# Interaction tower on one core: unrolled, row copies on VectorE, dots spread over the pairs, MLP feature by feature

## The reference

```python
e = stack([tbl_f[ids[:, f]] for f in range(32)], axis=1)   # [512, 32, 256], float32
z = einsum('bnd,bmd->bnm', e, e)[:, iu, ju]                # i < j: 496 dots per sample
h = concatenate([z, dense_ctx], axis=1)                    # 16 dense columns
h = maximum(h @ W_top1 + b_top1, 0)                        # 512
h = maximum(h @ W_top2 + b_top2, 0)                        # 256
y = h @ W_top3                                             # [512, 1]
```

## Time and profile before

| | us |
|---|---|
| median of 3 runs | 179.75 |
| lowest and highest | 179.70, 179.94 |
| profiled execution | 179.57 |
| its span | 177.8 |
| TensorE busy | 142.3 (80%) |
| GpSimd busy | 119.3 (67%) |
| VectorE, ScalarE busy | 61.5, 59.0 |

### The profile page before, as it was taken

How to read it: one execution, slowest core, us unless ns; L and a number is a source line. 1 busy time by engine, 2 the same in 40 slices (tenths; PEclk the granted TensorE clock), 3 DMA queues, 4 the chain that set the end, 5 groups by cost and what they waited for, 6 DMA issues and landing times.

```text
span 177.8 us, 3958 instructions
## 1 busy us (share of the span) xinstructions
PE 142.3 (80%) x1122; PEld 128.3 (72%) x1122; DVE 61.5 (35%) x185; ACT 59.0 (33%) x185; POOL 119.3 (67%) x131
## 2 busy tenths in 40 slices
PE   0387665797689999767689999767679999789995
PEld 0175554786569999646579999646579999678993
DVE  2101615045150255634140255534140255576202
ACT  2011415124150261533151162533151162565210
POOL 4777777777777777777777777777777777760000
PEclk9999999699999999999999999999999999999999
DMA  0356876533343333333333333333343333331000
GB/s 17 90 165 233 285 228 188 169 101 118 96 123 101 115 110 105 110 104 119 92 121 97 116 104 107 111 102 118 95 121 96 116 103 110 109 102 33 0 0 0
DMA packets 8801, 19.69 MB, mean 111 GB/s; under 512 B 2706, under 2 KB 3730, under 8 KB 8788
## 3 DMA queue, kind: packets, MB, share of 16 engines
q0 software_dynamic: 6000, 16.39, 31.0%
q10 hardware_dynamic: 1874, 2.69, 4.8%
q1 hardware_dynamic: 914, 0.46, 0.9%
HBM read 19.54 MB, written 0.00 MB: 110 GB/s over the span
## 4 chain that ended last, share of the span: by engine, by line
PE 51%; POOL 21%; DMA 14%; issue 9%; ACT 2%; DVE 1%; DVEq 0%; ACTq 0%
POOL rows L169 21%; PE gram_ps L191 18%; PE act_ps L239 12%; DMA rows<-tables,idx 10%; PE xt_ps L184 10%; PE dve_ps L239 4%; DMA w_sb<-w 3%; PE act_ps L250 2%; PE dve_ps L250 2%; PE act_ps L258 1%; PE xt_ps L234 1%; DMA ids_sb<-ids 1%; ACT xt L379 1%; DVE z L123 1%; ACT z L123 1%
## 5 line engine op out<-in xcount | busy, mean ns | idle before, releaser
L169 POOL DMA_INDIRECT rows<-tables,idx x125 | 118.6, 948 | 39.5 <-issue 29.6
L191 PE MATMUL gram_ps<-xt 128*128 128x128 f32 x512 | 71.4, 285 | 3.1 <-ACT xt L379 3.1
L184 PE MATMUL xt_ps<-ident,rows 128*128 128x128 f32 x250 | 47.5, 295 | 30.0 <-DMA rows<-tables,idx 26.5
L191 PEld LDWEIGHTS gram_ps<-xt 128*128 128x128 f32 x512 | 64.8, 199 | 4.8 <-ACT xt L379 4.0
L184 PEld LDWEIGHTS xt_ps<-ident,rows 128*128 128x128 f32 x250 | 29.0, 146 | 40.6 <-DMA rows<-tables,idx 29.2
L313 DVE COPY xt<-xt_ps 128x512 f32<-128x512 f32 x32 | 22.1, 692 | 83.8 <-PE xt_ps L184 83.5
L123 ACT COPY z<-gram_ps 32x64 f32 (+5 forms) x136 | 34.6, 254 | 36.1 <-PE gram_ps L191 34.7
L123 DVE COPY z<-gram_ps 32x64 f32 (+5 forms) x136 | 34.4, 253 | 6.4 <-PE gram_ps L191 4.7
L379 ACT COPY xt<-xt_ps 128x512 f32<-128x512 f32 x31 | 18.1, 584 | 54.1 <-PE xt_ps L184 53.9
L239 PE MATMUL act_ps<-z,w_sb 128*128 (+1 forms) x192 | 22.4, 277 | 0.3 <-DVE z L123 0.3
L239 PEld LDWEIGHTS act_ps<-z,w_sb 128*128 128x128 f32 x192 | 21.7, 192 | 0.9 <-issue 0.5
(11 more groups left out here) (18 smaller groups left out, 11.4 us busy)
## 6 DMA issues: line engine op xcount, KB each, us to landing
sp_rows<-tables SPq DMA_DIRECT2D x384, 1.0 KB
w_sb<-w ACTq DMA_DIRECT2D x8, 256.0 KB, 3.4
rows<-tables,idx POOLq DMA_INDIRECT x125, 2.8
w_sb<-w ACTq DMA_DIRECT2D x1, 512.0 KB, 5.0
ids_sb<-ids SPq DMA_DIRECT2D x1, 64.5 KB, 1.9
z<-dense ACTq DMA_DIRECT2D x1, 64.0 KB
sp_ids_sb<-sp_ids ACTq DMA_DIRECT2D x1, 3.0 KB
vec_sb<-vectors ACTq DMA_DIRECT2D x1, 4.0 KB, 1.7
```

Of the source, the lines that this page charges most:

```text
L169: pool.indirect_dma_start(rows[:, g % STEP, :], None, tables, bass.IndirectOffsetOnAxis(idx[:, g:g + 1], 0)).then_inc(rows_landed[g % STEP ...
L184: last = nc.tensor.transpose(xt_ps[:, bank, place, P * k:P * (k + 1)], x[:, P * k:P * (k + 1)], ident[:])
L191: last = nc.tensor.matmul(gram_ps[:, n // HALF, n % HALF, :], x, x, start=(k == 0), stop=(k == CHUNKS - 1))
```

## The change

- The loops are gone: all 64 pairs are written out on TensorE, VectorE and ScalarE.
- VectorE copies the transposed rows of all pairs; ScalarE copies only the last group, 127. VectorE now has group 126.
- The dot copies of an octet are spread: three, three and two pieces behind the copies of the next octet's second, third and fourth pair, on both engines.
- The singly fetched groups are 43, 86 and 125. The row buffers are used in the order of the gathers.
- The MLP stands at a delay from a pair: block b's features go one per pair, from pair 16(b + 1) + 4 on, alternately in `act_ps` and `dve_ps`; layer two comes at 5 pairs' delay, y at 7. ScalarE has the relus of features 0 and 2, VectorE those of 1 and 3. y is now in `dve_ps`, and its two matmuls are in the other order, both behind VectorE's relu.
- 17 idle passes for 18. The dense rows are loaded at the start, the weights one slot per pair.

```diff
-SP_GROUPS = tuple(GROUPS - STEP + n for n in (2, 3, 13))
...
-IDLE_PASSES = 18
...
+SINGLE_GROUPS = (43, 86, 125)
...
+IDLE_PASSES = 17
+DVE_QUADS = (0, 1)
+ACT_QUADS = (2, 3)
+DVE_SHARE = ((0, 3), (3, 6), (6, 8), (8, 8))
+ACT_SHARE = DVE_SHARE
...
-        dve_ps = psum("dve_ps", [P, 2, BLOCK])
-        h1_ps = [act_ps[:, 0, :], act_ps[:, 1, :], act_ps[:, 2, :], dve_ps[:, 0, :]]
-        h2_ps = [act_ps[:, 3, :], dve_ps[:, 1, :]]
-        y_ps = act_ps[0:1, 0, :]
+        dve_ps = psum("dve_ps", [P, 4, BLOCK])
+        h1_ps = [act_ps[:, 0, :], dve_ps[:, 0, :], act_ps[:, 1, :], dve_ps[:, 1, :]]
+        h2_ps = [act_ps[:, 2, :], dve_ps[:, 2, :]]
+        y_ps = dve_ps[0:1, 3, :]
...
+            pieces = [(q, jq) for q in quads for jq in range(QUADS)][part[0]:part[1]]
...
+        def stage_of(pair, delay):
+            b, at = divmod(pair - delay - OCTET_PAIRS, BLOCK_PAIRS)
+            return b - 1 if at == 0 and 1 <= b < BLOCKS else None
...
+                    pool.wait_ge(transposed, GATHERED[n - RING] + 1)
...
-                pe.wait_ge(xt_act if p % 2 else xt_dve, PAIRS // 2 * s + p // 2 + 1)
...
+                pe.wait_ge(xt_ready, pair + 1)
...
+                if m == 0 and b:
+                    pe.wait_ge(h2_act, b)
+                elif m == 1 and b:
+                    pe.wait_ge(y_copied, b)
+                elif m >= 2:
+                    pe.wait_ge(h1_dve if m % 2 else h1_act, 2 * b + 1)
...
             def y_all(b):
-                for m in range(N2):
-                    pe.wait_ge(h2_dve if m else h2_act, b + 1)
-                    last = nc.tensor.matmul(y_ps[:, :], w3[:, m:m + 1], h2[:, m, :],
-                                            start=(m == 0), stop=(m == N2 - 1))
+                if b == 0:
+                    pe.wait_ge(vec_loaded, 16)
+                pe.wait_ge(h2_dve, b + 1)
+                for m in reversed(range(N2)):
+                    if m == 0:
+                        pe.wait_ge(h2_act, b + 1)
+                    last = nc.tensor.matmul(y_ps, w3[:, m:m + 1], h2[:, m, :],
+                                            start=(m == N2 - 1), stop=(m == 0))
                 last.then_inc(y_done, 1)
...
+            def mlp_at(pair):
+                for stage, delay in ((h1_first, 0), (lambda b: h1_part(b, 1), 1), (lambda b: h1_part(b, 2), 2),
+                                     (lambda b: h1_part(b, 3), 3), (h2_all, 5), (y_all, 7)):
+                    b = stage_of(pair, delay)
+                    if b is not None:
+                        stage(b)
...
+            for pair in range(1, PAIRS - 1):
+                transpose_pair(pair)
+                gram_pair(pair - 1)
+                mlp_at(pair)
...
+            def copy_pair(pair):
+                dve.wait_ge(transposed, 2 * pair + 2)
+                nc.vector.tensor_copy(xt[:, pair % 2], xt_ps[:, pair % 2]).then_inc(xt_ready, 1)
...
+            for pair in range(PAIRS - 1):
+                copy_pair(pair)
+                if pair == 2:
+                    dve.wait_ge(vec_loaded, 16)
+                octet, at = divmod(pair - 1, OCTET_PAIRS)
+                if octet >= 1 and at < OCTET_PAIRS - 1:
+                    last = dots(OCTET * (octet - 1), OCTET, DVE_QUADS, DVE_SHARE[at])
+                    if at == OCTET_PAIRS - 2:
+                        last.then_inc(z_dve, 1)
+                mlp_at(pair)
+            dots(GROUPS - 2 * OCTET, OCTET, DVE_QUADS, DVE_SHARE[2]).then_inc(z_dve, 1)
+            octet = GROUPS - OCTET
+            dots(octet, OCTET // 2, (0, 1), (0, 4))
+            dve.wait_ge(transposed, GROUPS - 1)
+            nc.vector.tensor_copy(xt[:, 1, 0], xt_ps[:, 1, 0]).then_inc(xt_ready, 1)
+            dots(octet, OCTET // 2, (0, 1), (4, 8))
+            dots(octet + OCTET // 2, OCTET // 2, (0, 1), (0, 8)).then_inc(z_dve, 1)
...
+            act.dma_start(z[0:FIELDS, 0, :], dense).then_inc(dense_loaded, 16)
+            def load_weights(pair):
+                if pair < SLOTS:
+                    act.wait_ge(transposed, 2 * pair + 2)
+                    act.dma_start(w1_sb[:, pair, :], w1[:, pair, :]).then_inc(w1_loaded, 16)
+                elif pair == SLOTS:
+                    act.dma_start(w2_sb[:], w2.rearrange("(k p) n -> p k n", p=P)).then_inc(w2_loaded, 16)
...
+            dots(octet, OCTET // 2, (2, 3), (0, 4))
+            act.wait_ge(transposed, GROUPS)
+            nc.scalar.copy(xt[:, 0, 0], xt_ps[:, 0, 0]).then_inc(xt_act, 1)
+            dots(octet, OCTET // 2, (2, 3), (4, 8))
+            dots(octet + OCTET // 2, OCTET // 2, (2, 3), (0, 8)).then_inc(z_act, 1)
...
```

More of the change, by code:

```diff
@@ L109, in tower_kernel, with copy_dots, fetch_rows @@
         y_done = sem("y_done")
-        y_free = sem("y_free")
+        y_copied = sem("y_copied")
         y_stored = sem("y_stored")
         z_by_quad = z[:].rearrange("p s (g q) -> p q g s", q=QUADS)
[L115 to L125, removed]
-            return last
+        def copy_dots(copy, quads, first, count, part):
+            o, at = first // OCTET, first % OCTET
+            pieces = [(q, jq) for q in quads for jq in range(QUADS)][part[0]:part[1]]
+            for q, jq in pieces:
+                lo = 1 if jq == 0 else 0
+                j0 = FIELDS * q + SLOTS * jq
+                last = copy(
+                    z_by_quad[FIELDS * jq:FIELDS * (jq + 1), q, first:first + count, lo:SLOTS],
+                    gram_ps[FIELDS * q:FIELDS * (q + 1), o % 2, at:at + count, j0 + lo:j0 + SLOTS])
+            return last
+        def fetch_rows(engine, kind, lo, hi):
+            _, starts = nc.values_load_multi_w_load_instructions(
+                row_at[:, lo:hi], engines=[kind], min_val=0, max_val=(tables.shape[0] - 1) * ROW_BYTES,
+                skip_runtime_bounds_check_because="each DMA checks its own address against the table's end")
+            for n, start in enumerate(starts):
+                group, p = divmod(lo + n, P)
+                yield engine.dma_start(single_u8[p:p + 1, group, :], tables_u8[bass.ds(start, ROW_BYTES)]
+                                       ).then_inc(single_landed[group], 16)
+        def stage_of(pair, delay):
+            b, at = divmod(pair - delay - OCTET_PAIRS, BLOCK_PAIRS)
+            return b - 1 if at == 0 and 1 <= b < BLOCKS else None
         block = ctx.enter_context(nc.Block())
@@ L132, in _ @@
             sp.dma_start(ids_sb[:], ids).then_inc(ids_loaded, 16)
[L135 to L147, removed]
+            sp.wait_ge(row_at_ready, 1)
+            for lo in range(0, SP_ROWS, LOAD):
+                for _ in fetch_rows(sp, mybir.EngineType.SP, lo, min(lo + LOAD, SP_ROWS)):
+                    pass
+            sp.wait_ge(y_copied, BLOCKS)
             sp.dma_start(y.rearrange("b o -> o b"), y_row[:]).then_inc(y_stored, 16)
@@ L193, in gram_group, with transpose_pair @@
                 return last
[L195 removed]
+            def transpose_pair(pair):
                 for place in range(2):
[L197 to L209 removed]
```

333 lines of the change are left out of this document (138 added, 195 removed).

## The result

The changed kernel takes 180.16 us (median of 18 runs, 180.06 to 180.29), the one before 179.85 on the same chips (18 runs, 179.70 to 180.02). The ratio is 1.0017, 95% interval 1.0010 to 1.0024: slower by 0.31 us, 0.18 to 0.43. The forecast was 180.2 with a shift of 0.45.

The account below looks back on a forecast made before the run. The prediction took the gathers' cadence plus the serial tail as the bound. Its terms, 0.21 and 0.24, made +0.45 us on 179.57, so 180.02; placed on the 179.75 median, 180.2, own range 180.0 to 180.6, overall 179.5 to 181.0.

Parts of the forecast that it names:

- The bound: Whole kernel: GpSimd's 125 gathers, 1.2505 us each, then the serial tail set the end; mid-program waits are hidden.
- VectorE's chain: Tail: nine dot pieces (2.23 us) delay VectorE's copy of group 126 to 162.52; last block's layer one starts 0.21 later.
- The y order: Last MLP block: both y matmuls now wait for VectorE's relu, adding 0.24 us that nothing hides.
- The sum: Whole kernel: 0.21 for the tail before layer one plus 0.24 for the y product, +0.45 us.
- the two tail terms: After the last gather: layer one of the last block 0.21 us later, and the y product 0.24 us longer.
- the prediction's own line: Measurement: differences under about 0.2% (0.36 us) cannot be told from no change; slower means above 180.11.
- The 57% for a slowdown that can be told: Whole kernel: chance given to a measured time above 180.11, beside 35% for same and 8% for faster.
- Group 127 is no obstacle: Tail: group 127 lands at 161.39 and idle ScalarE has copied it by 162.3.
- the landing of 126 at 160.13: Tail: group 126 lands 2.84 us after its issue at 157.29 and stands transposed by 160.7, waiting for VectorE.
- the 0 for the unrolled code: Three engines' written-out instruction streams: no cost, or up to 0.3 us if one pause falls in the tail.
- The rival of a faster kernel: Tail: TensorE goes through groups 126 and 127 as they land, Gram 0.6 us earlier, 179.4 in all; 7%.
- The rule of the lock: Gathers: VectorE's 31 additional copies lock GpSimd out, 21 us more, 201 in all; 3%.

Follow-up runs that it names:

- a1: The changed kernel run again without any edit, beside the variants on the same chip; ratio to the kernel before 1.0031, median 180.48 us.
- b2: The changed kernel with the odd pairs' copies back on ScalarE up to pair 55; ratio to the kernel before 1.0027.
- b4: The changed kernel with the MLP of block 2 three pairs later; 182.49 us, ratio to the kernel before 1.0142.
- b3: The kernel before with only the new y product (VectorE's bank, both matmuls behind VectorE's relu); ratio to the kernel before 1.0014.
- a2: The changed kernel with y back in ScalarE's bank and its two matmuls in the old order; ratio to the kernel before 1.0011.
- a4: The changed kernel with old y order, Gram pair 62 ahead of group 126's transposes, and ScalarE copying both last groups; 179.64 us, ratio to before 0.9987.
- a3: The changed kernel with VectorE's four short dot pieces of groups 120 to 123 moved behind its copy of group 126; ratio to before 1.0006.
- c1: The changed kernel with 48 extra, useless VectorE copies from SBUF to SBUF; ratio to before 0.9687, on a chip where every kernel took 230 to 247 us.
- c4: The changed kernel with only Gram pair 62 moved ahead of group 126's transpose; 234.44 us beside 245.68 for the kernel before, on a slow chip.

## Why the prediction was right, point by point

- **The bound.** Right. The gathers come at an unbroken pace in both kernels, and everything in mid-program is hidden: a1 and b2 show it for the copies, the TensorE group for its waits, b4 for how far the cover reaches. Group 43 was laid out as wanted at 60.5; its first weight load is at 60.6, without a wait.
- **VectorE's chain.** Nine pieces between the copy of pair 62 and that of group 126: 2.23 laid out, 2.23 measured; the copy at 162.52 plus the 0.16 by which the last gather was later, 162.68, against 162.72. Layer one was laid out at +0.21. Behind the last gather it stands at 7.28 and 7.38 in the two traces with the old tail (before, b3) and at 7.55, 7.52, 7.51 and 7.44 in the four with the new one (changed, a1, a2, b2): 0.06 to 0.27 more, 0.18 between the means.
- **The y order.** +0.24 laid out, 0.22 measured, with the edit made and undone.
- **The sum.** 0.45 laid out; the two tail terms measure 0.22 + 0.2 in the traces, and the medians give 0.31 (0.18 to 0.43). The first pair of traces differs by 0.65 because the cadence differed by another 0.18 of spread. That 180.2 met 180.16 so closely is luck in part: the forecast stood on a median of 179.75, the kernel before measured 179.85 beside the changed one, and this 0.10 made up for most of the 0.14 by which the shift was too large. By the prediction's own line, 0.2% or 0.36 us, a shift of 0.31 could not be told from none; only the 18 runs of each kernel made it clear. The 57% for a slowdown that can be told was put just above a coin's, and the result lies at that edge.
- **What was wrong.** "Group 127 is no obstacle", the landing of 126 at 160.13, and the 0 for the unrolled code. Group 126 stood in its buffer only at 161.23, 3.77 after its issue, not 2.84, so that Gram pair 62, queued behind its transpose, waited too, and ScalarE copied group 127 at 162.82 and not by 162.3. It cost nothing here only because VectorE's chain ended at the same time. The 2.84 of group 124 was carried over to 126, and the unrolled code was given a cost of 0, or 0.3 as a pause in an engine's own stream; what the traces show is a landing some 1 us late beside a packet of instructions. The rival of a faster kernel rested on the same landing; a4, which shortens both chains, has that gain in its trace; a3, which shortens VectorE's alone, has not.
- **The rule of the lock.** Rightly given 3%: it does not hold for copies out of PSUM (a1, b2), though it does, weakly, for those from SBUF (c1). The prediction let it cover the 31 copies by rule, though the case that the section names is a copy from SBUF to SBUF and these read PSUM.

## What to carry to other kernels

When one engine has an unbroken cadence, count from its last item to the end and ignore the waits before, however many the change removes, as long as the others have caught up when that item lands (b4). In the tail, write down every chain that meets at the last product: two that are equal hide each other, and an edit to one alone may show nothing. Of two matmuls that make one sum, the one that waits for the slower input should stand last; the other order, chosen for a bank, cost 0.22 us here. Written-out code is not free where a landing decides: look in the profile for when its instructions are loaded, and which transfer is then in flight.

## What the runs showed of the hardware

- A gather lands 2.7 to 2.9 us after its issue for the most part, but after 3.3 to 4.5 us in 38 of the 40 cases in which a 16 KB packet of queue q8, "instruction", started 1.1 to 2.3 us behind its issue. The last gather but one was such a case in all eight traces of the unrolled program (transposed 3.72 to 4.55 us after its issue in the six in which TensorE stood waiting for it), and so was the one transposed at 56.00 in the changed kernel.
- The stretch of 123 gathers and pauses differs by 0.22 us between two executions of the same kernel and by 0.37 over the ten traces; the whole effect measured here is 0.31.
- A VectorE copy of 0.42 us from SBUF to SBUF lengthens a gather that begins while it runs by 0.05 to 0.24 us, if at least 0.19 us of the copy is still to come; one from PSUM does not.
- On one chip the same programs took 230 to 247 us in place of 180, with pauses in several engines' instruction streams: TensorE's ahead of its Gram matmuls were up to 15.8 us long and 54.6 us in sum in c4.
